# Condition weights loaded, mixed and masked in column halves, with early products of 256 columns into cleared banks

## What is computed

```python
def cond(x, y, weight, mask, bias):                 # x (2,2048,512), y (2,8), weight (8,512,512)
    w_bot = einsum('bg,got->bot', y, weight * mask)  # one 512x512 matrix per batch
    return einsum('bnt,bot->bno', x, w_bot) + bias
def bitlinear(x, w):                                 # int8-like rows of x, ternary w
    return einsum('bsi,oi->bso', act_quant(x), weight_quant(w))
def ffn(x, w_gate, w_up, w_down):                    # inner size 2048
    return bitlinear(silu(bitlinear(x, w_gate)) * bitlinear(x, w_up), w_down)
out = x + ffn(cond(x, cond_8, cond_weight, cond_mask, cond_bias), w_gate, w_up, w_down)
```

## Time and profile before

| | before |
|---|---|
| median of 3 runs | 453.29 us (452.04 to 454.02) |
| the profiled execution's own time | 453.42 us |
| its span in the trace | 451.6 us |
| TensorE busy | 434.9 us, 96% |
| VectorE busy | 366.4 us, 81% |
| ScalarE busy | 327.1 us, 72% |
| GpSimd busy | 154.4 us, 34% |
| granted clock of TensorE | full (2.4 GHz) over the span |

### The profile page before, as it was taken

How to read it: one execution, slowest core, us unless ns; L and a number is a source line. 1 busy time by engine, 2 the same in 40 slices (tenths; PEclk the granted TensorE clock), 3 DMA queues, 4 the chain that set the end, 5 groups by cost and what they waited for, 6 DMA issues and landing times.

```text
span 451.6 us, 7215 instructions
## 1 busy us (share of the span) xinstructions
PE 434.9 (96%) x2186; PEld 232.7 (52%) x2186; DVE 366.4 (81%) x625; ACT 327.1 (72%) x448; POOL 154.4 (34%) x160
## 2 busy tenths in 40 slices
PE   4899998999999999999999999999999999999995
PEld 0234443444444455555655555655556565555654
DVE  0316579898956798799998999999999989999991
ACT  1216847785356776888888888888888888888861
POOL 0000170606099554232424324233341434414122
PEclk9999999999999999999999999999999999999999
DMA  7999997995420434352634526345353553535455
GB/s 281 402 401 415 412 252 160 339 279 121 102 48 10 78 77 109 103 116 77 159 69 134 119 75 150 67 133 118 91 134 75 141 107 103 116 93 142 86 148 139
DMA packets 104458, 69.78 MB, mean 155 GB/s; under 512 B 87281, under 2 KB 87537, under 8 KB 102897
## 3 DMA queue, kind: packets, MB, share of 16 engines
q1 hardware_dynamic: 103856, 67.39, 54.3%
q10 hardware_dynamic: 576, 2.10, 1.3%
HBM read 40.11 MB, written 8.39 MB: 107 GB/s over the span
## 4 chain that ended last, share of the span: by engine, by line
PE 44%; DMA 23%; DVE 12%; issue 11%; ACT 8%; SPq 1%; DVEq 0%; ACTq 0%
PE ps L888 12%; DMA wc<-wc 12%; PE ps L843 10%; PE ps L951 8%; PE ps L923 7%; DMA wc<-w_gate 4%; PE ps L881 4%; ACT wc L473 4%; DVE wc L733 3%; DVE wc L699 3%; DMA qT<-q_sb 3%; DMA wc<-wcond 2%; DMA wc<-w_down 2%; DVE p_part L751 2%; PE ps L856 1%
## 5 line engine op out<-in xcount | busy, mean ns | idle before, releaser
L888 PE MATMUL ps<-tern_up,qT 128*128 128x512 f16 x512 | 131.2, 379 | 0.6 <-DVE wc L733 0.6
L843 PE MATMUL ps<-w_bot,xT_sb 128*128 128x512 f32 x256 | 113.2, 595 | 2.3 <-DVE w_bot L636 1.6
L843 PEld LDWEIGHTS ps<-w_bot,xT_sb 128*128 128x128 f32 x256 | 48.0, 190 | 61.2 <-issue 57.5
L751 DVE TENSOR_REDUCE p_part<-wc 128x1 f32<-128x1536 f32 x64 | 77.9, 1218 | 1.7
L888 PEld LDWEIGHTS ps<-tern_up,qT 128*128 (+1 forms) x512 | 50.0, 98 | 55.3 <-DVE wc L733 1.3
L733 DVE TENSOR_TENSOR wc<-ps,xT_sb 128x512 f32<-128x512 f32 x104 | 71.3, 685 | 7.5 <-issue 3.6
L473 ACT ACTIVATE wc<-wc 128x1024 f16<-128x1024 f32 x64 | 67.0, 1051 | 4.6 <-DVE wc L796 2.8
L463 ACT ACTIVATE wc<-wc,p_scale 128x2048 f32<-128x2048 f32 x31 | 62.1, 2002 | 4.5 <-DVE p_scale L789 4.5
L951 PE MATMUL ps<-wc 128*128 128x256 f16 x480 | 62.2, 273 | 0.2 <-DVE wc L699 0.2
L699 DVE TENSOR_TENSOR wc<-wc 128x1024 f16<-128x1024 f16 x60 | 56.7, 945 | 3.8 <-DMA wc<-wc 2.7
L458 ACT ACTIVATE xT_sb<-ps,gate_unit 128x512 f32<-128x512 f32 x78 | 49.2, 684 | 11.7 <-PE ps L923 11.2
(11 more groups left out here) (93 smaller groups left out, 544.1 us busy)
## 6 DMA issues: line engine op xcount, KB each, us to landing
xT_sb<-xT SPq DMA_DIRECT2D x32, 256.0 KB, 7.5
x_res<-x SPq DMA_DIRECT2D x30, 256.0 KB, 2.9
out<-result SPq DMA_DIRECT2D x30, 256.0 KB, 2.4
wc<-wcond SPq DMA_DIRECT2D x12, 512.0 KB, 13.6
wc<-w_gate SPq DMA_DIRECT2D x4, 1024.0 KB, 17.7
wc<-w_up SPq DMA_DIRECT2D x4, 1024.0 KB, 13.4
wc<-w_down SPq DMA_DIRECT2D x4, 1024.0 KB, 7.3
wc<-wcond ACTq DMA_DIRECT2D x4, 512.0 KB, 7.7
```

Of the source, the lines that this page charges most:

```text
L751: nc.vector.tensor_reduce(p_part[:, par, i:i + 1], prod[:, par, 512 * lo:512 * hi], AX.X, ALU.max, apply_absolute_value=True).then_inc(par ...
L843: ins = nc.tensor.matmul(ps[:, t % COND_BANKS], xT_sb[:, t % XSLOTS, k], w_bot[:, t // HALF, k], start=(k == 0), stop=(k == KH - 1))
L888: ins = nc.tensor.matmul(ps[:, UP + i % 2], tile_of(s, k), tern_up[:, i, k], start=(k == 0), stop=(k == KH - 1))
```

## The change

1. The condition weight lies in DRAM and in `wc` with its 512 columns in two halves h of 256 (`parts`). A half slice is 1 MB in two DMAs of 512 KB, each with four of the eight blocks of 256 columns; before, a DMA held two blocks of 512.
2. `mix_products(n)`, the copies, the merges and the masks of batch 0 run for n = 0 to 7, that is for k = n // 2 and the column half n % 2, on 256 columns each.
3. `early_products(n, tiles)` adds a product of 256 columns. Its matmuls never start a group (`start=False`), so the banks of tiles 0 to 5 are set to zero by VectorE ahead (`clear_banks`, two instructions of three banks).
4. SP loads tiles 0 to 5 of xT ahead of the slices 1 to 3 of `wc`.
5. Pieces 0 and 1 of `w_gate` are issued after the products of slices 0 and 1 are mixed, pieces 2 and 3 after three tiles of xT, which wait for the first tiles' products; the first four transpositions stand between the pieces of `w_up`. `AHEAD` is 11 instead of 12.
6. ScalarE sums `w_gate` pieces 2 and 3 after its rounding of tiles 1 and 2; before, all four pieces came ahead of tile 0.
7. `SUM_TILE` is (9, 15, 23) instead of (8, 14, 21), `mean_after` 4, 11, 21 instead of 5, 11, 19, and the pieces of `w_up` and `w_down` are clipped from tiles 16 and 24 on instead of 15 and 23.

```diff
--- before.py
+++ after.py
@@ -27,7 +27,7 @@
 LATE = TILES - 2
-AHEAD = 12
+AHEAD = 11
 HSLOTS = 3
 QSLOTS = 4
-SUM_TILE = (8, 14, 21)
-SUM_BANK = (10 % 8, 16 % 8, 23 % 8)
+SUM_TILE = (9, 15, 23)
+SUM_BANK = (11 % 8, 17 % 8, 25 % 8)
 ROUND = 12582912.0
@@ -69,2 +69,3 @@
         wc = sb("wc", [P, KH, BLOCKS, HID], F32)
+        parts = wc[:, :].rearrange("p k g n -> p (k g n)").rearrange("p (k h g n) -> p k h g n", k=KH, h=2, g=BLOCKS)
         raw_a = wc[:, 0:2].rearrange("p k g n -> p (k g n)").rearrange("p (a n) -> p a n", a=PIECES)
...
@@ -206,6 +208,5 @@
 
-            def load_wc(k):
-                for i in range(4 if k > 0 else 0):
-                    sp.dma_start(wc[:, k, 2 * i:2 * i + 2], wcond[k, :, 2 * i:2 * i + 2]).then_inc(s_wc[k][i], 16)
-                load_mask(0, k)
+            def load_wc(k, h):
+                for i in range(2):
+                    sp.dma_start(parts[:, k, h, 4 * i:4 * i + 4], wcond[k, h, :, 4 * i:4 * i + 4]).then_inc(s_wc[k][h][i], 16)
 
@@ -219,10 +220,9 @@
             sp.dma_start(y_sb[:, :], y_col).then_inc(s_small, 16)
-            load_wc(0)
-            for t in range(FIRST):
-                load_xT(t)
-            load_wc(1)
-            for t in range(FIRST, EARLY):
+            load_mask(0, 0)
+            for t in range(EARLY):
                 load_xT(t)
-            load_wc(2)
-            load_wc(3)
+            for k in range(1, KH):
+                load_wc(k, 0)
+                load_mask(0, k)
+                load_wc(k, 1)
             for t in range(EARLY, XSLOTS):
@@ -230,19 +230,25 @@
             sp.dma_start(bias_sb[:, :], bias.partition_broadcast(P)).then_inc(s_bias, 16)
-            for a in range(PIECES):
-                if a % 2 == 0:
-                    sp.wait_ge(mix_psum, 2 * (a // 2 + 1))
-                load_raw(0, w_gate, a)
-            for a in range(PIECES):
-                if a % 2 == 0:
-                    sp.wait_ge(mix_psum, 2 * (a // 2 + 3))
-                if a == 0:
-                    for t in range(XSLOTS, XSLOTS + 3):
-                        load_xT(t)
-                if a == 2:
-                    for k in range(KH):
-                        load_mask(1, k)
-                    for t in range(XSLOTS + 3, AHEAD):
-                        load_xT(t)
-                load_raw(1, w_up, a)
-            for t in range(LATE):
+            sp.wait_ge(mix_psum, 8)
+            load_raw(0, w_gate, 0)
+            load_raw(0, w_gate, 1)
+            for t in range(XSLOTS, XSLOTS + 3):
+                load_xT(t)
+            load_raw(0, w_gate, 2)
+            load_raw(0, w_gate, 3)
+            load_xT(XSLOTS + 3)
+            sp.wait_ge(mix_psum, 4 * KH)
+            load_raw(1, w_up, 0)
+            transpose_q(0)
+            load_raw(1, w_up, 1)
+            transpose_q(1)
+            for k in range(KH):
+                load_mask(1, k)
+            load_xT(XSLOTS + 4)
+            transpose_q(2)
+            load_raw(1, w_up, 2)
+            load_xT(XSLOTS + 5)
+            transpose_q(3)
+            load_raw(1, w_up, 3)
+            load_xT(XSLOTS + 6)
+            for t in range(QSLOTS, LATE):
                 if t + AHEAD < TILES:
...
@@ -580,4 +586,5 @@
 
-            for i in range(4):
-                nc.scalar.dma_start(wc[:, 0, 2 * i:2 * i + 2], wcond[0, :, 2 * i:2 * i + 2]).then_inc(s_wc[0][i], 16)
+            for h in range(2):
+                for i in range(2):
+                    nc.scalar.dma_start(parts[:, 0, h, 4 * i:4 * i + 4], wcond[0, h, :, 4 * i:4 * i + 4]).then_inc(s_wc[0][h][i], 16)
             act.wait_ge(s_small, 16)
@@ -585,10 +592,11 @@
             act.wait_ge(half_ready, 1)
-            for k in range(KH):
-                act.wait_ge(mix_psum, 2 * k + 1)
+            for n in range(2 * KH):
+                k, cut = n // 2, slice(NB * (n % 2), NB * (n % 2) + NB)
+                act.wait_ge(mix_psum, 2 * n + 1)
                 for b in range(BATCH):
-                    nc.scalar.activation(w_bot[:, b, k], ps[:, MIX], ACT.Copy, scale=half_on[:, b:b + 1]
+                    nc.scalar.activation(w_bot[:, b, k, cut], ps[:, MIX, cut], ACT.Copy, scale=half_on[:, b:b + 1]
                                          ).then_inc(half_copied, 1)
-            for a in range(PIECES):
-                abs_sum_piece(0, a)
-            abs_after = {3: (1, 0), 4: (1, 1), 5: (1, 2), 6: (1, 3), 12: (2, 0), 13: (2, 1), 14: (2, 2), 15: (2, 3)}
+            abs_sum_piece(0, 0)
+            abs_sum_piece(0, 1)
+            abs_after = {1: (0, 2), 2: (0, 3), 3: (1, 0), 4: (1, 1), 5: (1, 2), 6: (1, 3), 12: (2, 0), 13: (2, 1), 14: (2, 2), 15: (2, 3)}
             for t in range(LATE):
@@ -614,2 +622,3 @@
                                         ALU.add).then_inc(half_ready, 1)
+                clear_banks(0, 3)
                 dve.wait_ge(s_small, 16)
@@ -621,17 +630,22 @@
 
-            def merge_halves(k):
-
+            def clear_banks(lo, hi):
+                nc.vector.memset(ps[:, lo:hi], 0.0).then_inc(banks_zero, 1)
 
+            def merge_halves(n):
+                k, cut = n // 2, slice(NB * (n % 2), NB * (n % 2) + NB)
                 for b in range(BATCH):
-                    dve.wait_ge(mix_psum, 2 * k + 2)
-                    dve.wait_ge(half_copied, 2 * k + b + 1)
-                    nc.vector.scalar_tensor_tensor(out=w_bot[:, b, k], in0=ps[:, MIX + 1], scalar=half_on[:, 1 - b:2 - b],
-                                                   in1=w_bot[:, b, k], op0=ALU.mult, op1=ALU.add).then_inc(half_merged, 1)
+                    dve.wait_ge(mix_psum, 2 * n + 2)
+                    dve.wait_ge(half_copied, 2 * n + b + 1)
+                    nc.vector.scalar_tensor_tensor(out=w_bot[:, b, k, cut], in0=ps[:, MIX + 1, cut], scalar=half_on[:, 1 - b:2 - b],
+                                                   in1=w_bot[:, b, k, cut], op0=ALU.mult, op1=ALU.add).then_inc(half_merged, 1)
                     if b == 0:
-                        apply_mask(0, k, w_bot0_ready)
-
-            def apply_mask(b, k, done):
-                dve.wait_ge(half_merged, 2 * k + b + 1)
-                dve.wait_ge(s_mask[b][k], 16)
-                nc.vector.tensor_tensor(w_bot[:, b, k], w_bot[:, b, k], mask_sb[:, b, k], ALU.mult).then_inc(done, 1)
+                        dve.wait_ge(half_merged, 2 * n + 1)
+                        dve.wait_ge(s_mask[0][k], 16)
+                        nc.vector.tensor_tensor(w_bot[:, 0, k, cut], w_bot[:, 0, k, cut], mask_sb[:, 0, k, cut], ALU.mult
+                                                ).then_inc(w_bot0_ready, 1)
+
+            def apply_mask(k):
+                dve.wait_ge(half_merged, 4 * k + 4)
+                dve.wait_ge(s_mask[1][k], 16)
+                nc.vector.tensor_tensor(w_bot[:, 1, k], w_bot[:, 1, k], mask_sb[:, 1, k], ALU.mult).then_inc(w_bot1_ready, 1)
 
@@ -798,7 +812,8 @@
             mix_weights()
-            for k in range(KH):
-                merge_halves(k)
+            clear_banks(3, EARLY)
+            for n in range(2 * KH):
+                merge_halves(n)
             dve.wait_ge(s_bias, 16)
-            mean_after = {5: 0, 11: 1, 19: 2}
-            piece_after = {first + a: (m, a) for m, first in enumerate((7, 15, 23)) for a in range(PIECES)}
+            mean_after = {4: 0, 11: 1, 21: 2}
+            piece_after = {first + a: (m, a) for m, first in enumerate((7, 16, 24)) for a in range(PIECES)}
             for t in range(LATE):
@@ -807,3 +822,3 @@
                     for k in range(KH):
-                        apply_mask(1, k, w_bot1_ready)
+                        apply_mask(k)
                 if t in piece_after:
@@ -847,6 +862,7 @@
 
-            def mix_products(k):
-                if k > 0:
-                    pe.wait_ge(half_copied, 2 * k)
-                    pe.wait_ge(half_merged, 2 * k)
+            def mix_products(n):
+                k, h = n // 2, n % 2
+                if n > 0:
+                    pe.wait_ge(half_copied, 2 * n)
+                    pe.wait_ge(half_merged, 2 * n)
                 for half in range(2):
@@ -854,13 +870,19 @@
                         if half == 0:
-                            pe.wait_ge(s_wc[k][c], 16)
-                        ins = nc.tensor.matmul(ps[32 * c:32 * c + 32, MIX + half], mix_w[:, T16 * half:T16 * half + 32],
-                                               wc[:, k, 2 * c + half], start=True, stop=True)
+                            pe.wait_ge(s_wc[k][h][c // 2], 16)
+                        ins = nc.tensor.matmul(ps[32 * c:32 * c + 32, MIX + half, NB * h:NB * h + NB],
+                                               mix_w[:, T16 * half:T16 * half + 32], parts[:, k, h, 2 * c + half],
+                                               start=True, stop=True)
                     ins.then_inc(mix_psum, 1)
 
-            def early_products(k, tiles):
-                pe.wait_ge(w_bot0_ready, k + 1)
+            def early_products(n, tiles):
```

(34 more changed lines are left out.)

## The result

The changed kernel is slower: 456.21 us median of 20 runs (453.44 to 459.42) against 452.84 of the kernel before, measured beside it (20 runs, 451.54 to 456.05). The ratio is 1.0073, 95% interval 1.0055 to 1.0091. That is 3.4 us more, where 3.4 less were forecast. The execution that was profiled took 459.0 us, with a span of 457.2; it is the third longest of the 20, so its waits stand for the long runs more than for the median.

A forecast was written before the change was run, and what follows sets the result against it. TensorE, busy 96% of the span, was taken as the bound, with idle time at the start and at 71 to 80 us. Gains of 1.5 and 1.87 sum to 3.4 us, from 453.42 to 450.0; range 448.5 to 453.5.

The forecast's parts named there:

- Two rounds of two records of 0.43 become two of 0.215: At the start, half the columns save 0.86 us of mixing behind the landing; first product at 10.35 instead of 15.64.
- I take half, 0.43: Early products on TensorE: a 256-column product takes 0.43 us, half of 0.86.
- the 1.5 us: Gain at the start: early products end at 41.1 instead of 42.65 us.
- A mixing block: At the start, a 256-column mixing block takes 1.18 us instead of 2.04, within bounds of 1.02 and 2.04.
- Rivals B: A fixed part in each of 48 added product records, up to 0.07 us each: 453.4 us; chance 0.10.
- C: Mixing block stays at 2.04 us, set by its loads and starts, not its columns: 455.5 us; chance 0.08.
- The queue is still busy with piece 1 until 41.15, so the wait itself is hidden: SP's wait at tile 8 of xT for the first complete tile, 0.7 us later, would not delay w_gate 2 and 3.
- rival A: New wait of 1 to 3 us at `abs_total(0)`, from late w_gate or xT transfers: 451 to 453 us; chance 0.20.
- the fit of 0.3 us: ScalarE finishes w_gate piece 3 near 51.1, TensorE reaches `abs_total(0)` at 51.4 us.
- Both waits go: TensorE's waits at the second `abs_total` and at the tile behind it vanish: 1.23 + 0.64 = 1.87 us.
- I count no new wait for TensorE: VectorE's later w_down mean costs it about 1.7 us, but it starts some 2.8 us earlier, so TensorE is not delayed.
- Behind it nothing changes: First gate product moves from 128.53 to about 125.1 us; everything after it stays the same.

The follow-up runs named there:

- experiment 14: Kernel before plus 56 one-column f32 matmuls with one-column weights, half ahead of the first mixing block and half behind it (224 instructions): 455.34 us, ratio 1.0041.
- experiment 11: Changed kernel plus 8 one-column f32 matmuls (32 instructions) ahead of the first mixing block: 455.65 us, ratio 1.0070.
- experiment 8: 256-column head with the old order behind it, plus 8 f32 matmuls of zeros keeping TensorE busy at the start: 453.77 us, ratio 1.0015.
- Experiments 10: Changed kernel with w_gate 2 and 3 issued ahead of the x tiles, plus 8 one-column matmuls (32 instructions): 452.17 us, ratio 0.9987.
- 12: Changed kernel with w_gate 2 and 3 ahead of the x tiles, 8 one-column matmuls, means behind tiles 5, 11, 19, w_down's sum ahead of tile 21: 451.16 us.
- experiment 3: Old 512-column head of the kernel before, with the changed kernel's order behind it: 452.44 us, ratio 0.9999.
- experiment 4: Kernel before with two unused 2048-column reductions on VectorE behind tile 28: 456.92 us, ratio 1.0085.
- 2: Changed kernel's 256-column head with the kernel before's order of loads, sums and means behind it: 455.32 us, ratio 1.0061.
- 7: Changed kernel with w_gate 2 and 3 issued right behind 0 and 1, plus 32 empty TensorE instructions: 453.92 us.
- experiments 9: Kernel before plus 56 one-column f32 matmuls with 128-column weights (224 instructions) ahead of the first mixing block: 470.66 us.
- 6: 256-column head with the old order behind it, plus 32 empty instructions ahead of TensorE's first matmul: 456.23 us.
- 1: Changed kernel with w_gate 2 and 3 issued ahead of the three x tiles: 453.34 us, ratio 1.0009.

## Why the prediction was wrong

**Where the 3.4 us come from.** By medians 456.21 falls to 453.34 when w_gate 2 and 3 are issued early (-2.9), and to 452.17 when the last fetch is also moved back (-1.2). These two costs, 4.0 us, stand against a gain of 0.7 in the rest. On the kernel before, the moved fetch costs 2.5 (experiment 14). The split is one of medians and depends on the order of the steps: moving the fetch alone gave 0.6 (experiment 11), within the spread of its runs. Much of both costs is the clock: of the changed kernel's 20 runs eight had a mean granted clock of 0.999 (median 455.5), nine 0.994 to 0.996 and three, at 457.9 to 459.4, 0.990 or 0.991.

**The first product and the head.** The first step that failed is the price of the early records. "Two rounds of two records of 0.43 become two of 0.215" and "I take half, 0.43" a product hold at the higher clock only, and I took the clock of the earlier trace rows for the new start. There the first product, at 15.64, stood behind 14 mixing records on end. In the changed kernel TensorE had done 16 short records with waits of 1.6 and 1.05 between them, and ran on at the lower level until 16 us. So the first product came at 10.97 and not 10.35, the second block ended at 15.69 and not 14.14, and the early products at 42.57 and not 41.1: the 1.5 us were lost by 15.69, and of the forecast gain 0.1 was left at the end of the start (42.65 before). The Trainium skill (TensorE: Matmul & The Clock Gate, section What's actually happening) says that the throttled clock is the default and activity releases it; experiment 8 agrees, with 1.46 against 2.93 us for the same six records. The granted clock of the windows reads 1.00 at the start, in the kernel before too, so the lower level shows there in the durations only.

**A mixing block and a record** were right: from the third block on a block with its changes takes 1.21 (1.18 forecast), and records stand 0.214 apart (0.215). Rivals B and C, which made these dear, fell. No run here shows the overhead on each matmul that the Trainium skill states (TensorEngine Tiling, section Instruction Overhead): 20 records take 4.58 us, which is 19 x 0.215 and 0.49 from the last start to its modelled end.

**"The queue is still busy with piece 1 until 41.15, so the wait itself is hidden"** failed. The landing was read from before's trace. In the changed kernel piece 1 landed at 40.1, and the wait ended at 40.72, since tile 0 was complete 1.47 later than I had it. DMAs issued at 42.04 landed 7.9 us later in the profiled execution. This was rival A in its mechanism ("the transfers of w_gate 2 and 3 start late"), with 2.09 us at `abs_total(0)`. I priced it at 1 to 3 us and gave it a fifth of the chance; the fit of 0.3 us deserved more.

**Both waits go** was right, and so was the count that the earlier transposition frees ScalarE (issued at 46.01, not 44.5). **"I count no new wait for TensorE"** failed: VectorE started late by the 6.22 at the mean and met 2.80 at GpSimd's scaling (1.7 forecast), and its lateness came out at the third gate chunk, 2.82 and a fallen clock. Experiments 10 and 12 show what VectorE's waits are worth: with 3.89 at the mean and 2.5 at the scaling of w_down the third chunk waits 1.06; in 12, with 2.18 at the mean, 2.04 at the scaling of w_gate and none at that of w_down, it waits not at all, and the time falls by 1.0.

**"Behind it nothing changes"** failed, and I had no rival for it. The head's 112 more records and their loads (2298 against 2186 of each) moved the last instruction fetch from 0.1 us behind the issue of a pair of transpositions to 2.7 us behind it, between the two. What that costs is 0.7 in waits and, in the runs in which the clock falls behind the wait, 1.7 more.

## What to carry to other kernels

When work is cut into more instructions, look where the instruction fetches of a tight tail fall in the trace, and compare the rows of the tail before and after; here 32 instructions more took 0.6 to 1.8 us away again (experiments 10 and 11). When work at the start is made shorter, look up at which clock its records ran, and whether the new order leaves TensorE idle between them; here records priced at 0.215 took 0.43 and more until 16 us. And a load that stands behind a wait in a queue is hidden only as long as the transfers ahead of it last in the new kernel, not in the old one: put the load that the critical engine needs ahead of the wait. And one profiled execution is one draw: here two executions with the same order of loads waited 2.82 and 1.06 us at the same place.

## What the runs showed of the hardware

With a fetch of 0.02 MB of instructions between the two DMA transpositions of a pair, TensorE waited 2.07 us for it and not 0.40, and the next wait fell from 0.99 to nothing. Empty instructions moved the fetch by some 0.5 us at most, real matmuls moved it further: with 224 more it started 2.6 to 2.7 us behind the issue, with 256 more at most 0.6. One-column f32 matmuls cost 0.22 us a record with 128-column weights at the start (3.57 us for 16) and 0.03 with one-column weights (1.54 for 56).

Waits of 2.64, 2.82 and 2.83 us of TensorE (experiment 3, the changed kernel, experiment 4) were each followed by the clock at its lower level; 16 records behind a wait of 2.07, 2.11 or 2.12 (experiments 14, 2 and 7) took 5.31 us and not 3.63. Behind 2.08, 2.11, 2.13 and 2.13 (experiments 9, 6, 1 and the changed kernel) they took 3.63, and behind 1.06 and 1.08 the clock stayed at 1.00. So at 2.1 us the same wait has both outcomes, in executions of the same kernel too, as the runs of 14 show.
